# A Mamba layer's projections, moved to other steps of the scan loop

## The reference

```python
xz = x @ W_in                                  # 256 -> 1024
xc, z = jnp.split(xz, 2, axis=-1)              # 512 channels each
xc = silu(causal_conv4(xc) + conv_b)
proj = xc @ W_xproj                            # 512 -> 48: dt_r (16), B (16), C (16)
dt = softplus(dt_r @ W_dt + b_dt)
dA = exp(dt[..., None] * A)                    # 512 channels x 16 states
dBx = (dt * xc)[..., None] * Bm[:, :, None, :]
h = h * dA_t + dBx_t; y = einsum('ben,bn->be', h, C_t)   # over the 1024 tokens
y = (y + xc * D) * silu(z)
x = x + y @ W_out
```

## Time and profile before

| | us |
|---|---|
| median of the runs | 3112.89 |
| the profiled execution, its own time | 3112.89 |
| its span, first to last instruction | 3111.3 |
| of it the Mamba stage, about | 1000 |

### The profile page before, as it was taken

The page is one execution under the profiler, slowest core; times in us unless marked ns, Lnnn a source line. Parts: engine busy times, 40 slices in busy tenths (PEclk is TensorE's granted clock), DMA queues, the critical chain, the costliest instruction groups (busy, mean ns, idle before and its releaser), DMA issues. The chain is left out here.

```text
span 3111.3 us, 41107 instructions
## 1 busy us (share of the span) xinstructions
PE 2805.9 (90%) x14082; PEld 1830.9 (59%) x14082; DVE 2043.9 (66%) x3705; ACT 1473.0 (47%) x2768; POOL 1510.9 (49%) x1192
## 2 busy tenths in 40 slices
PE   7899999999986876999999999888859999999998
PEld 2343343343333664556666666566648888888887
DVE  7899999999899744577777777577852222222222
ACT  6677677677663400367667767555521111111111
POOL 5698898898786554133443343267651111111111
PEclk8899999999999878999999999999969999999999
DMA  7145045045050064213322222211116555666652
GB/s 240 36 128 164 22 144 162 17 149 155 17 166 0 32 185 132 86 31 83 85 71 69 69 51 70 54 45 43 49 67 227 186 186 189 195 200 200 198 185 61
DMA packets 283853, 346.30 MB, mean 111 GB/s; under 512 B 85787, under 2 KB 238551, under 8 KB 283591
## 3 DMA queue, kind: packets, MB, share of 16 engines
q1 hardware_dynamic: 260399, 310.17, 32.4%
q0 software_dynamic: 16704, 27.21, 3.7%
q10 hardware_dynamic: 6544, 6.30, 0.7%
HBM read 234.69 MB, written 107.95 MB: 110 GB/s over the span
## 5 line engine op out<-in xcount | busy, mean ns | idle before, releaser
L542 POOL TENSOR_TENSOR mb_drive<-mb_dtx,mb_b_rep 128x1024 f32<-128x1024 f32 x255 | 596.4, 2360 | 155.9 <-DVE mb_pD L439 77.4
L861 PE MATMUL mb_pY<-mb_hc,ident 128*128 128x512 f32 x1024 | 499.1, 612 | 51.5 <-DVE mb_hc L456 51.1
L2022 DVE TENSOR_REDUCE at_nm_of<-at_pR 128x1 f32<-128x512 f32 (+3 forms) x640 | 379.2, 632 | 88.1 <-PE at_pR L2011 44.1
L3188 POOL DMA_INDIRECT out<-et_y,et_to x71 | 112.0, 1577 | 660.9 <-DVE et_y L3242 413.6
L3232 DVE TENSOR_TENSOR et_mT<-et_silu,et_pU 128x512 f32<-128x512 f32 (+1 forms) x160 | 100.3, 627 | 473.8 <-ACT et_silu L3203 473.8
L3203 ACT ACTIVATE et_silu<-et_pG 128x512 f32<-128x512 f32 (+1 forms) x160 | 87.9, 549 | 652.2 <-PE et_pU L3264 652.2
L861 PEld LDWEIGHTS mb_pY<-mb_hc,ident 128*128 128x128 f32 x1024 | 189.6, 193 | 322.3 <-issue 196.6
L598 ACT ACTIVATE mb_pD<-mb_dt,mb_a_neg 128x512 f32<-128x512 f32 x384 | 260.3, 689 | 126.0 <-DVE mb_hc L456 113.7
L439 DVE TENSOR_TENSOR_SCAN mb_pD<-mb_pD,mb_drive 128x1024 f32<-128x1024 f32 x128 | 292.7, 2288 | 39.7 <-ACT mb_pD L596 37.4
L445 DVE TENSOR_TENSOR_SCAN mb_pD<-mb_pD,mb_carried,mb_drive 128x512 f32<-128x512 f32 x256 | 314.1, 1268 | 4.5 <-ACT mb_pD L598 4.0
L456 DVE TENSOR_TENSOR mb_hc<-mb_pD,mb_c_rep 128x1024 f32<-128x1024 f32 x256 | 307.9, 1203 | 0.0
(11 more groups left out here) (486 smaller groups left out, 4936.2 us busy)
## 6 DMA issues: line engine op xcount, KB each, us to landing
t_wg<-in_t_wgT SPq DMA_DIRECT2D x40, 1024.0 KB, 6.0
t_wu<-in_t_wuT SPq DMA_DIRECT2D x40, 1024.0 KB, 8.6
t_wd<-in_t_wdT SPq DMA_DIRECT2D x40, 1024.0 KB, 11.2
mb_b_rep<-mb_rows SPq DMA_DIRECT2D x64, 512.0 KB, 3.7
mb_c_rep<-mb_rows SPq DMA_DIRECT2D x64, 512.0 KB
t_h_sorted<-blank SPq DMA_DIRECT2D x6, 4160.0 KB, 19.9
t_h_sorted<-blank SPq DMA_DIRECT2D x18, 1170.0 KB, 6.3
t_h_sorted<-blank SPq DMA_DIRECT2D x12, 1040.0 KB, 6.1
```

Source lines behind the costliest of these rows:

```text
L542: nc.gpsimd.tensor_tensor(drive[G % RINGS][:, :, :], dtx[:, m, :].unsqueeze(1).to_broadcast([P, 2, CH]), b_rep[:, 2 * j:2 * j + 2, :], ALU ...
L861: last = nc.tensor.matmul(pY[:, :], K.ident[:, :], hc[G % RINGS][:, k, :], start=False, stop=(j == PAIRS - 1 and k == 1))
L2022: nc.vector.tensor_reduce(nm_of[t % 2][:, w0 // 512, sides[0]:sides[0] + m, qb], bank("S", t, k)[:, 0:m * w].rearrange("p (a w) -> p a w", ...
```

## The change

The arithmetic is the same. The steps in which PE makes the pieces and ACT reads them are different, and with them `ORDER`:

- CV0 of the next chunk goes from steps 1 and 2 (5 and 6 in chunk 0) to 10 and 11, CV3 from 13, 14 to 12, 13, XC1 from 12 to 14, CV2 from 18, 19 to 19, 20. Z0 of the next chunk goes from 10 to 21.
- PROJ goes from 21, 22 (read in 22) to 23, 24 (read in 24), LN0 and LN1 from 24 and 25 to 18 and 22.
- DT0 goes from 23 to 25, DT2 from 31 to 28. DT1 stays in 26, XC0 and XC3 of the chunk after next in 29 and 30.
- ACT's two Silu groups stand in steps 9 and 21, where they were in 11 and 20. In a chunk between the first and the last the group of step 11 had four gates and one tile (5 operations) and that of step 20 three tiles; now step 9 has three gates and step 21 four tiles and one gate.
- `small` and `rounded` of DT0 stand both in step 25 (were 23 and 24), `small` of DT1 and both logarithms in 26 (were 26 and 27), `rounded` of DT1 in 27 (was 28), `small` of DT2 in 28 (was 31). Of the tiles 2 and 3 `rounded` stands in steps 2 and 3 (was 1 and 5) and the logarithms in 4 (was 3).

```diff
@@ def mamba
     for i in range(NCH):
         ORDER += [("DT3", i)]
-        ORDER += [("CV0", i + 1)] * (0 < i < LAST) + [("O0", i - 1), ("O1", i - 1)] * (i > 0)
-        ORDER += [("XC0", 1), ("XC3", 1), ("Z0", 0), ("CV0", 1)] * (i == 0)
+        ORDER += [("O0", i - 1), ("O1", i - 1)] if i > 0 else [("XC0", 1), ("XC3", 1), ("Z0", 0)]
         ORDER += [("Z1", i), ("Z2", i), ("Z3", i)]
         if i < LAST:
-            ORDER += [("Z0", i + 1), ("XC1", i + 1), ("CV3", i + 1), ("CV1", i + 1), ("XC2", i + 1), ("CV2", i + 1)]
-            ORDER += [("PROJ", i + 1), ("DT0", i + 1)] + [("LN0", i + 2), ("LN1", i + 2)] * (i + 1 < LAST) + [("DT1", i + 1)]
-            ORDER += [("XC0", i + 2), ("XC3", i + 2)] * (i + 1 < LAST) + [("DT2", i + 1)]
+            ORDER += [("CV0", i + 1), ("CV3", i + 1), ("XC1", i + 1), ("CV1", i + 1), ("XC2", i + 1)]
+            ORDER += [("LN0", i + 2)] * (i + 1 < LAST) + [("CV2", i + 1), ("Z0", i + 1)] + [("LN1", i + 2)] * (i + 1 < LAST)
+            ORDER += [("PROJ", i + 1), ("DT0", i + 1), ("DT1", i + 1), ("DT2", i + 1)]
+            ORDER += [("XC0", i + 2), ("XC3", i + 2)] * (i + 1 < LAST)
@@ ACT, behind the decays of a step
             def more_of(i, s):
-                if s == 0:
+                if s == 1:
                     small(i, 3)
-                if s == 1:
-                    rounded(i, 2)
-                if s == 3:
+                if s in (2, 3):
+                    rounded(i, s)
+                if s == 4:
                     logarithm(i, 2)
                     logarithm(i, 3)
-                if s == 5:
-                    rounded(i, 3)
-                if s == (11 if i > 0 else 9):
-                    silu_gates(i, range(1 if i > 0 else 0, ME))
-                    if 0 < i < LAST:
-                        silu_gates(i + 1, (0,))
-                        silu_inner(i + 1, (0,))
+                if s == 9:
+                    silu_gates(i, (1, 2, 3) if i > 0 else (0, 1, 2, 3))
                 if i < LAST:
-                    if s == 20:
-                        silu_inner(i + 1, (3, 1, 2) if i > 0 else (0, 3, 1, 2))
-                        if i == 0:
-                            silu_gates(1, (0,))
-                    if s == 23:
+                    if s == 21:
+                        silu_inner(i + 1)
+                        silu_gates(i + 1, (0,))
+                    if s == 25:
                         small(i + 1, 0)
-                    if s == 24:
                         rounded(i + 1, 0)
...
@@ PE, behind the state sum of a step
                     if i < LAST:
-                        if s == 10:
+                        if s in (10, 12, 15, 19):
+                            convolve(i + 1, {10: 0, 12: 3, 15: 1, 19: 2}[s], (0, 1))
+                        if s in (11, 13, 16, 20):
+                            convolve(i + 1, {11: 0, 13: 3, 16: 1, 20: 2}[s], (2, 3))
+                        if s in (14, 17):
+                            inner(i + 1, {14: 1, 17: 2}[s])
+                        if s == 18 and i + 1 < LAST:
+                            transpose(i + 2, 0)
+                        if s == 21:
                             gate(i + 1, 0)
...
+                        if s == 22 and i + 1 < LAST:
+                            transpose(i + 2, 1)
+                        if s == 23:
                             project(i + 1, (0, 1), True, False)
-                        if s == 22:
+                        if s == 24:
                             project(i + 1, (2, 3), False, True)
-                        if s in (23, 26, 31):
-                            step(i + 1, {23: 0, 26: 1, 31: 2}[s])
-                        if s in (24, 25) and i + 1 < LAST:
-                            transpose(i + 2, s - 24)
+                        if s in (25, 26, 28):
+                            step(i + 1, {25: 0, 26: 1, 28: 2}[s])
```

More of the change, by code:

```diff
@@ L629, in silu_gates, with silu_inner @@
                     nc.scalar.activation(yz(ch, m), yz(ch, m), ACT.Silu).then_inc(s_gate, 1)
-            def silu_inner(ch, tiles):
-                for m in tiles:
+            def silu_inner(ch):
+                for m in range(ME):
                     eng.wait_ge(s_read, use(f"CV{m}", ch))
@@ L682, in read_of @@
                     step(i, 3)
-                if i == 0 and s in (1, 2):
+                if s in (4, 6) and i > 0:
+                    summed(i - 1, s // 2 - 2)
+                if s in (1, 2) and i == 0:
                     inner(1, {1: 0, 2: 3}[s])
-                if i == 0 and s == 4:
+                if s == 6 and i == 0:
                     gate(0, 0)
[L687 to L690, removed]
                 if s in (7, 8, 9):
@@ L734, in more_of @@
                         small(i + 1, 1)
-                    if s == 27:
                         logarithm(i + 1, 0)
                         logarithm(i + 1, 1)
+                    if s == 27:
+                        rounded(i + 1, 1)
                     if s == 28:
-                        rounded(i + 1, 1)
-                    if s == 31:
                         small(i + 1, 2)
@@ L886, in _ @@
                         step(i, 3)
[L887 to L892, removed]
                     if s in (3, 4, 5, 6) and i > 0:
@@ L898, in _ @@
                         project_out(i - 1, s // 2 - 1 if s % 2 else s // 2 - 2, 1 - s % 2, range(ME))
+                    if s in (1, 2) and i == 0:
+                        inner(1, {1: 0, 2: 3}[s])
+                    if s == 6 and i == 0:
+                        gate(0, 0)
                     if s in (7, 8, 9):
@@ L906, in _ @@
                     if i < LAST:
[L907 to L915 removed]
+                        if s in (10, 12, 15, 19):
+                            convolve(i + 1, {10: 0, 12: 3, 15: 1, 19: 2}[s], (0, 1))
+                        if s in (11, 13, 16, 20):
+                            convolve(i + 1, {11: 0, 13: 3, 16: 1, 20: 2}[s], (2, 3))
+                        if s in (14, 17):
+                            inner(i + 1, {14: 1, 17: 2}[s])
+                        if s == 18 and i + 1 < LAST:
+                            transpose(i + 2, 0)
+                        if s == 21:
+                            gate(i + 1, 0)
+                        if s == 22 and i + 1 < LAST:
+                            transpose(i + 2, 1)
+                        if s == 23:
                             project(i + 1, (0, 1), True, False)
[L917 removed]
+                        if s == 24:
                             project(i + 1, (2, 3), False, True)
[L919 to L922 removed]
+                        if s in (25, 26, 28):
+                            step(i + 1, {25: 0, 26: 1, 28: 2}[s])
                         if s in (29, 30) and i + 1 < LAST:
```

22 lines of the change are left out of this document (4 added, 18 removed).

## The result

The changed kernel takes 3136.05 us, the median of 4 runs (3130.43 to 3142.54), against 3112.12 for the kernel before in the same series: a ratio of 1.0086 [1.0069, 1.0102], 24 us slower. In a later series it is 3134.25 against 3106.99, a ratio of 1.0069 [1.0051, 1.0087]. The direction was forecast. The size was not: 9 us were forecast, and 3136 lies outside the range.

What follows compares the result with a forecast made beforehand. VectorE was taken to set the pace, its waits nearly all for ACT's decays. Chunk terms 2.4 + 1.8 + 1.2 + 2.8 - 2.3 = +5.9 us, plus 3.5 for PE's clock, gave +9.4 on 3112.89: 3122 us, range 3107 to 3132.

Steps and rivals of the forecast that it cites:

- Silu group of step 21: Larger Silu group on ACT makes VectorE wait 3.1 us in even chunks, 1.1 in odd ones, 3.9 in chunk 0.
- Steps 25 to 28: Filled-up end of a chunk: ACT's late decays cost VectorE 3.5 us in even chunks, 0.8 in odd ones.
- Chunk 0: First chunk: its large wait moves, with weigh waiting 2.4 us for PE and 5.8 at item 13; +2.4 us in all.
- Logarithms in step 4: Even chunks: logarithms of tiles 2 and 3 with O0's read cost 0.7 us on item 7; 1.4 in chunk 6.
- Chunk 2 as a check: VectorE's waits in chunk 2 would be about 7.3 us, of it 3.1 at item 24 and 2.4 at item 29.
- PE's clock at XC0: PE idles ahead of XC0 for DT2's late read and may drop its clock: 0 to 8.4 us, taken as 3.5.
- The step that failed: PROJ's read, moved to step 24: PE idles at most about 0.5 us for it and no wait is left.
- slower by more: Rival at 3134 us, chance 0.10: PE's clock drops at every XC0 and in steps 26 and 27; late reads reach next chunk.

Runs made afterwards that it cites:

- The tail put alone into the kernel before: Kernel before with DT2 in step 28 ahead of XC0 and XC3, both logarithms in 26, rounded of DT1 in 27: 3135.26 us, ratio 1.0074.

## Why the prediction was right in sign and wrong in size

- **Silu group of step 21**: forecast 3.1 us in an even chunk and 1.1 in an odd one; measured 2.98 (2.49 in chunk 6, for which 2.6 was forecast) and 0.98. Right. In chunk 0, where 3.9 was forecast for a late Z0, it is 3.15: 0.8 too much.
- **Steps 25 to 28**: forecast 0.4, 2.4 and 0.7 us; measured 0.42, 2.41 and 0.58. In odd chunks 1.17 where 0.8 was forecast, together 1.1 us too little. The tail put alone into the kernel before costs 14.0 us of stage end and 22.8 of time.
- **Chunk 0**: forecast `weigh` 2.4 and item 13 5.8; measured 1.43 and 5.33 in the first trace, 2.25 and 5.75 in the second. Right in place, 1.4 us too much by the first.
- **Logarithms in step 4**: forecast 0.7 us in chunks 2 and 4 and 1.4 in chunk 6, 2.8 in all; measured 4.9 in steps 0 to 7 of these, 2.0 too little, of it 1.19 in one place of chunk 4.
- **Chunk 2 as a check**: 7.3 us of waits for decays were forecast, with "I am wrong if chunk 2's waits come out under 5 us"; those of the chunk are 0.83, 2.98 and 3.41, together 7.2.
- **PE's clock at XC0**: mis-sized. 3.5 us forecast, about 5.9 measured, inside 0 to 8.4. The slow ones cost 0.22 and 1.21 us in even chunks (forecast 1.1) and 2.93 and 1.56 in odd ones (1.7). Of the six waits of 2.75 us or more ahead of XC0 in the first trace, four were followed by slowed products (2.79, 3.78, 3.78 and 3.65 us for four rows) and two by 1.98. The Trainium skill (TensorE: Matmul & The Clock Gate, HAM oscillation), read as strictly as the prediction read it, would have all six slow; the trace agrees with four and not with the other two.
- **The step that failed**: "PROJ's read now stands two steps farther from the group (step 24), PE has idled at most about 0.5 us for it, and no wait is left there." I counted what PROJ needs (the four tiles after their Silu: 0.45 us, and that is what it waits once LN1 is out of the way) and not what stands ahead of it in the bank. LN1's read was counted on ACT, where it costs 0.5 us, and not as the release of PE's next turn. PE idled 3.5 to 3.7 us in even chunks and 2.9 in odd ones, in five of the six places the products behind it ran in part at 1.2 GHz, and the finish of step 25 waited 13.9 us in six chunks. The experiment with LN1 in 27 takes away 12.5 us of stage end and 11.3 of time; the one that puts LN1 back into a kernel with PROJ late costs 7.2 of stage end, of which about 5.6 belong to the order.

The sum: forecast +9.4 us; with 13.9 for the finish, 2.4 more of the clock, 1.1 more in odd chunks, 2.0 more in steps 0 to 7, and 2.2 less in chunk 0 it is +26.6, against a stage that grew by 27.9; 1.0 of that is a first scan at 40.70 in place of 39.71. The agreement is partly chance: VectorE's waits of 0.2 us and more grew by 24.6, and the 2.3 us that are then left stand in no such wait. The rival "slower by more", at 3134, came near the time by luck: it had the clock fall at every XC0, which came in four of six places of the first trace, and the wait of the finish is not among what it named. Its chance of 0.10 was too small mainly since the count of waits stopped at ACT and VectorE. Two small readings: the 0.2 us put between `weigh` and ACT is about 0.03 in the rows of before (`weigh` ends at 390.98, keep starts at 391.01), and the 8.28 us of the earlier trace rows are 6.85 in the second trace. The time did not move outside the Mamba stage by the change as far as the traces show: from the stage end to the end of the span it is 2111.6 and 2112.0 us before and 2101.1 and 2108.9 after, and the 2101.1 holds the short form of the last section.

## What to carry to other kernels

When several producers share one bank in a fixed order, the price of moving a piece is not only its own inputs: for each turn, ask who reads the piece before it, and what that reader has in front of it. A small read behind a long group on its engine blocks the next large product. Move a piece and its neighbours in the order together: PROJ a step later was worth 13.7 us of stage end when LN1 was put behind it. With LN1 ahead of it about half of that was gone, and in the changed kernel, where the group ahead of LN1's read is larger too, LN1's place cost 12.5.

## What the runs showed that was not expected

- The same idle time of PE is followed by either clock level in different executions of one kernel: ahead of PROJ, 3.52 us in chunk 2 of the changed kernel gave 3.14 us for four rows in one trace and 1.92 in the other. In the two traces of the changed kernel PE waits 2.75 us or more ahead of PROJ or XC0 24 times, and behind 17 of these the products were slowed, for about 1.5 to 3 us over the two groups of four rows. So a wait here costs its length and, about three times in four, that much more.
- The cross-attention stage has two lengths, whatever the Mamba stage is: 319.4 and 318.1 us in the traces of before, 307.5 and 316.9 in those of after. In the long form PE idles over 6 us near its end for a read by ACT and the router's products behind it run at half clock. Of the traces of all thirteen runs eight have the long form (4.9 to 6.7 us idle) and five the short one (0.8). The changed kernel's first trace fell on the short form, which hides 12 us of its loss: by spans alone it would be only 17 us slower. The row in the long form (before) and in the short one (after):

```profile
2299.17 3.55 PE L3053 MATMUL xa_pT<-xc_router,xa_hT 128*128 128x8 f32 x16 [6.71 <-ACT xa_hT L2913]
```

```profile
2319.77 1.92 PE L3045 MATMUL xa_pT<-xc_router,xa_hT 128*128 128x8 f32 x16 [0.82 <-ACT xa_hT L2905]
```

- Chips differ by more than the change: the kernel before is 3112.49, 3097.22 and 3106.99 us in three series. Times can be compared only as ratios within a series. For stage ends, chunks 1, 3 and 5 are 118.5 us long in the run with chunk 0's finish earlier, on the fastest chip, and 118.5 in before's first trace. What makes the chips differ stays open; a part of it may be the form of the cross-attention stage, since all four traces from the fastest chip have the short one.
